# A normalised 3x3 convolution over 32 images: the order of work inside an image's slot, and the start of image 0

## The reference

```python
# x: (32, 128, 56, 56) float32; weight (128, 128, 3, 3); Wp, Wn: (1,); bias (128,)
w_norm = weight / max|weight|;  delta = 0.05 * max|w_norm|
tern = 1 where w_norm > delta, -1 where w_norm < -delta, else 0
wq = Wp * tern where tern > 0, Wn * tern where tern < 0, else 0
g = x in 32 groups of 4 channels, each normalised over its 4*56*56 values, eps 1e-5
out = x + conv3x3(g, wq, stride 1, padding 1) + bias
```

## Time and profile before

| | |
|---|---|
| median of 3 executions | 548.46 us (548.22 to 550.05) |
| the profiled execution | 549.22 us, span 547.5 us |
| busy, share of the span | TensorE 95%, VectorE 96%, ScalarE 87%, GpSimd 28% |
| transfers | 152.6 MB, mean 279 GB/s |
| image 0: sum complete on VectorE (second half of plane C) | 10.76 us |
| last store issued | 543.1 us |

### The profile page before, as it was taken

The page is one execution under the profiler, slowest core; times in us unless marked ns, Lnnn a source line. Parts: engine busy times, 40 slices in busy tenths (PEclk is TensorE's granted clock), DMA queues, the critical chain, the costliest instruction groups (busy, mean ns, idle before and its releaser), DMA issues. The chain is left out here.

```text
span 547.5 us, 9220 instructions
## 1 busy us (share of the span) xinstructions
PE 522.0 (95%) x3171; PEld 308.2 (56%) x3171; DVE 525.3 (96%) x448; ACT 475.8 (87%) x483; POOL 154.5 (28%) x138
## 2 busy tenths in 40 slices
PE   1898999999999999999999999999999999999995
PEld 0454655556555555655555555555555555555553
DVE  4999999999999999999999999999999999999985
ACT  2879999999989999899999999899998999999841
POOL 2313332232333223233322233322223332222320
PEclk9998999999999999999999999999999999999999
DMA  7535999999999999999999999999999999998766
GB/s 277 235 119 157 294 282 276 272 267 280 362 260 313 306 286 281 367 269 304 295 306 286 295 335 251 343 304 271 287 354 279 297 321 275 273 305 222 194 191 258
DMA packets 27959, 152.61 MB, mean 279 GB/s; under 512 B 3488, under 2 KB 3488, under 8 KB 27936
## 3 DMA queue, kind: packets, MB, share of 16 engines
q1 hardware_dynamic: 18576, 102.77, 48.3%
q0 software_dynamic: 8784, 48.98, 45.8%
q10 hardware_dynamic: 576, 0.59, 0.3%
HBM read 100.94 MB, written 51.38 MB: 278 GB/s over the span
## 5 line engine op out<-in xcount | busy, mean ns | idle before, releaser
L841 PE MATMUL even_rows<-parts,w_lhsT 128*128 128x392 f16 (+1 forms) x1536 | 265.8, 329 | 4.3 <-DVE parts L679 1.9
L841 PE MATMUL odd_rows<-parts,w_lhsT 128*128 128x392 f16 (+1 forms) x1536 | 263.3, 327 | 1.9 <-ACT d_sb L430 1.7
L841 PEld LDWEIGHTS even_rows<-parts,w_lhsT 128*128 128x128 f16 x1536 | 150.0, 99 | 105.9 <-issue 6.9
L841 PEld LDWEIGHTS odd_rows<-parts,w_lhsT 128*128 128x128 f16 x1536 | 147.3, 97 | 110.4 <-issue 11.8
L672 DVE SCALAR_TENSOR_TENSOR parts<-plane,norm_scale,parts 128x1568 f16<-128x1568 f32 x111 | 203.5, 1843 | 1.6 <-ACT parts L439 1.5
L349 POOL TENSOR_TENSOR plane<-x 128x756 f32<-128x756 f32 x64 | 97.4, 1522 | 343.3 <-DVE plane L609 115.9
L439 ACT ACTIVATE parts<-plane,norm_scale 128x1568 f16<-128x1568 f32 x111 | 177.7, 1601 | 9.2 <-ACT plane L473 4.9
L478 ACT ACTIVATE junk<-x,negmean 128x3136 f16<-128x3136 f32 x32 | 92.7, 2898 | 0.0
L424 ACT ACTIVATE c_sb<-even_rows,bias_sb,out_scale 128x1568 f32<-128x1568 f32 x32 | 53.1, 1659 | 15.9 <-PE even_rows L841 15.9
L387 POOL DMA_DIRECT2D y<-in_x_dram x61 | 54.2, 988 | 31.2 <-DVE y L689 29.4
L689 DVE SCALAR_TENSOR_TENSOR y<-odd_rows,out_scale,c_sb 128x1568 f32<-128x1568 f32 x31 | 57.4, 1853 | 2.2 <-issue 1.3
(11 more groups left out here) (67 smaller groups left out, 132.9 us busy)
## 6 DMA issues: line engine op xcount, KB each, us to landing
x<-in_x_dram SPq DMA_DIRECT2D x64, 784.0 KB, 12.0
out_dram<-y SPq DMA_DIRECT2D x63, 784.0 KB, 6.2
y<-in_x_dram POOLq DMA_DIRECT2D x61, 784.0 KB, 12.1
out_dram<-y SPq DMA_DIRECT2D x2, 392.0 KB, 3.7
y<-in_L_conv_weight_dram ACTq DMA_DIRECT2D x1, 576.0 KB, 6.5
wp_sb<-in_L_conv_Wp_dram ACTq DMA_DIRECT2D x1, 0.5 KB, 7.6
wn_sb<-in_L_conv_Wn_dram ACTq DMA_DIRECT2D x1, 0.5 KB, 7.9
bias_sb<-in_L_conv_bias_dram ACTq DMA_DIRECT2D x1, 0.5 KB, 7.8
```

The costliest lines, as they stand in the source:

```text
L841: ins = nc.tensor.matmul(product_ps(odd, b, b + 1)[:, 0, r0 - b * BANK_ROWS:r1 - b * BANK_ROWS, :], w_lhsT[:, prod, kh, :], part(img, prod ...
```

## The change

Every engine's slot gets another order, and slots -1 and 0 too.
- TensorE: the statistics matmul of n+1 (with the mean of n+2) moves from ahead of product C to between products D and A of slot n. It waits for the copy of C (`c_ready`), the squares of n+1 and the sum of n+2. Bank 3 of A waits for the root's and the mean's readers, no longer bank 3 of C.
- VectorE: the slot begins with low D of n (it was the last of slot n-1), then odd rows of n-1, low A, plane C of n+2 (it was of n+3), low B, reciprocal, D of n+1, Newton, A of n+1, scale, even rows of n, low C of n+1.
- ScalarE: squares of n+1, high B, copy of C, root of n+1, mean of n+2, copy of D, centre, high C, high D, edges and high A of n+1. The casts of the turned weights A and B move here from VectorE, into slot 0.
- GpSimd: the first half of plane B waits for plane A of that image alone; for image 0 for its sum instead of its root. The second half always waits for low D.
- Slot -1: the mean of image 1 gets a matmul of its own (`sum_second_mean`) behind the turned weights, so that the variance of image 0 no longer waits for plane C of image 1; only the weights C are turned ahead of it. The first half of plane D comes ahead of plane C of image 1, the output scales move to slot 0, the edges ahead of the root, and there are 7 warm-up matmuls instead of 6.

```diff
 PSUM_BANK = 512
-WARM_UP = 6
+WARM_UP = 7
...
@@ -351,27 +352,20 @@
         if h:
             ins.then_inc(plane_ready[B], 1)
-    def first_half_b(img, now, third):
+    def first_half_b(img, now):
         pool.wait_ge(x_loaded[img.buf], img.turn * 32 + 32)
         wait(pool, lo_ready[B], img.count())
         if now:
             wait(pool, product_done[A], now.half(1, 1, 1))
-            if now.j == 0:
-                pool.wait_ge(plane_ready[A], img.count(plus=1))
-            elif third:
-                pool.wait_ge(sum_ready, third.count(plus=1))
-            else:
-                pool.wait_ge(plane_ready[A], img.count(plus=1))
+            pool.wait_ge(plane_ready[A], img.count(plus=1))
         else:
-            pool.wait_ge(std_ready, img.count(plus=1))
+            pool.wait_ge(sum_ready, img.count(plus=1))
         difference_b(img, 0)
     def second_half_b(img, prev):
         if prev:
             wait(pool, product_done[B], prev.half(1, 1, 1))
-            pool.wait_ge(lo_ready[D], img.count(plus=1))
-        else:
-            pool.wait_ge(plane_ready[A], img.count(plus=1))
+        pool.wait_ge(lo_ready[D], img.count(plus=1))
         difference_b(img, 1)
...
         if nxt:
-            first_half_b(nxt, now, third)
-
-    slots(p, pool, emit, ahead=4)
+            first_half_b(nxt, now)
+
+    slots(p, pool, emit)
...
 nc.scalar.activation(root_of_zero[:], no_bias[:], ACT.Sqrt)
 def run(p):
+    def copy_turned_weights(js):
+        for j in js:
+            wait(act, product_done[j], p * N_IMG * HALVES)
+            act.wait_ge(w_turned, 4 * p + j + 1)
+            nc.scalar.activation(w_lhsT[:, j].rearrange("p k c -> p (k c)"), turned_ps(j),
+                                 ACT.Copy).then_inc(last_w_ready, 1)
+
...
             nc.scalar.activation(first_rows(part(img, C, HI), h), first_rows(plane_of(img, C), h), ACT.Copy,
                                  scale=norm_scale[:, b_slice(img)]).then_inc(ready, 1)
-    def take_mean(img):
-        if img.j == 0:
-            act.wait_ge(mean_summed, p + 1)
+    def take_mean(img, first=False):
+        if first:
+            act.wait_ge(mean_summed, 2 * p + img.j + 1)
...
@@ -490,43 +491,30 @@
     def emit(prev, now, nxt, far):
         first_slot, second_slot = not now and not prev, now and not prev
         if first_slot:
-            take_mean(nxt)
+            take_mean(nxt, first=True)
             sum_squares(nxt)
+            edges(nxt)
+            root(nxt)
             centre(nxt)
-            root(nxt)
-            take_mean(far)
-            edges(nxt)
             make_first_hi(nxt)
+            take_mean(far, first=True)
             make_hi(nxt, D)
-        elif second_slot:
-            sum_squares(nxt)
-            make_hi(now, A)
+        elif now:
+            if second_slot:
+                copy_turned_weights((A, B))
+                make_hi(now, A)
+            if nxt:
+                sum_squares(nxt)
+            make_hi(now, B)
             copy_c(now)
-            make_hi(now, B)
-            root(nxt)
-            take_mean(far)
-            copy_d(now)
-            centre(nxt)
-            make_hi(nxt, C)
-            make_hi(nxt, D)
-            sum_squares(far)
-            edges(nxt)
-            make_hi(nxt, A)
-        elif now:
             if nxt:
                 root(nxt)
             if far:
                 take_mean(far)
+            copy_d(now)
             if nxt:
                 centre(nxt)
-            make_hi(now, B)
-            copy_c(now)
-            if nxt:
                 make_hi(nxt, C)
-            if far:
-                sum_squares(far)
-            copy_d(now)
-            if nxt:
                 make_hi(nxt, D)
                 edges(nxt)
...
                             apply_absolute_value=True).then_inc(w_max_local, 1)
 def ternary_weights():
+    dve.wait_ge(scalars_loaded, 32)
+    nc.vector.tensor_tensor(equal[:], wp_sb[:], wn_sb[:], ALU.is_equal).then_inc(w_step, 1)
+    steps[0] += 1
     dve.wait_ge(w_max_turned, 1)
     step(nc.vector.tensor_reduce(w_max[:], w_max_ps, AX_X, ALU.max))
     nc.vector.tensor_scalar(above[:], w_max[:], THRESHOLD, None, ALU.mult)
-    nc.vector.tensor_scalar(below[:], w_max[:], -THRESHOLD, None, ALU.mult).then_inc(w_step, 1)
-    steps[0] += 1
-    dve.wait_ge(scalars_loaded, 32)
-    step(nc.vector.tensor_tensor(equal[:], wp_sb[:], wn_sb[:], ALU.is_equal))
+    step(nc.vector.tensor_scalar(below[:], w_max[:], -THRESHOLD, None, ALU.mult))
     step(nc.vector.tensor_scalar(neg, w_raw, below[:], equal[:], ALU.is_lt, ALU.mult))
     nc.vector.scalar_tensor_tensor(pos, w_raw, above[:], neg, ALU.is_gt, ALU.subtract).then_inc(w_ternary, 1)
...
@@ -726,61 +714,50 @@
             make_first_c(nxt, 1)
             if p == 0:
                 ternary_weights()
-                output_scales()
+            make_first_d(nxt, 0)
             make_c(far)
-            make_first_d(nxt, 0)
+            rstd_of_x(nxt)
             turned_weights((C, D))
-            rstd_of_x(nxt)
             make_first_d(nxt, 1)
             make_first_lo(nxt)
-        elif second_slot:
-            make_a(now)
+        elif now:
+            if second_slot:
+                make_a(now)
             make_lo(now, D)
-            turned_weights((A, B))
+            if prev:
+                output_rows(prev, ODD)
+            if second_slot and p == 0:
+                output_scales()
             make_lo(now, A)
-            make_c(far)
+            if far:
+                make_c(far)
+            if second_slot:
+                make_d(nxt)
             make_lo(now, B)
-            make_d(nxt)
-            first_rstd(nxt)
-            make_a(nxt)
-            newton_factor(nxt)
-            scale_of_x(nxt)
-            output_rows(now, EVEN)
-            make_lo(nxt, C)
-            make_lo(nxt, D)
-            make_c(third)
-        elif now and nxt:
-            output_rows(prev, ODD)
-            first_rstd(nxt)
-            make_lo(now, A)
-            newton_factor(nxt)
-            make_d(nxt)
-            scale_of_x(nxt)
-            make_lo(now, B)
-            make_lo(nxt, C)
-            make_a(nxt)
-            if third:
-                make_c(third)
-            output_rows(now, EVEN)
-            make_lo(nxt, D)
-        elif now:
-            output_rows(prev, ODD)
-            make_lo(now, A)
-            make_lo(now, B)
-            if p == 0:
-                add_half_residual(prev)
-            for odd in (EVEN, ODD):
-                add_last_residual(now, 0, odd)
-            last_output_rows(now, 0, 2, EVEN, first_rows_done[EVEN])
-            last_output_rows(now, 0, 2, ODD, first_rows_done[ODD])
-            for odd in (EVEN, ODD):
-                add_last_residual(now, 1, odd)
-            last_output_rows(now, 2, 3, EVEN, last_rows_done[EVEN])
-            last_output_rows(now, 2, 3, ODD, last_rows_done[ODD])
-            last_output_rows(now, 3, 4, EVEN, even_done)
-            last_output_rows(now, 3, 4, ODD, odd_done)
-
-    slots(p, dve, emit, ahead=4)
+            if nxt:
+                first_rstd(nxt)
+                if not second_slot:
+                    make_d(nxt)
+                newton_factor(nxt)
+                make_a(nxt)
+                scale_of_x(nxt)
+                output_rows(now, EVEN)
+                make_lo(nxt, C)
+            else:
+                if p == 0:
+                    add_half_residual(prev)
+                for odd in (EVEN, ODD):
+                    add_last_residual(now, 0, odd)
+                last_output_rows(now, 0, 2, EVEN, first_rows_done[EVEN])
+                last_output_rows(now, 0, 2, ODD, first_rows_done[ODD])
+                for odd in (EVEN, ODD):
+                    add_last_residual(now, 1, odd)
+                last_output_rows(now, 2, 3, EVEN, last_rows_done[EVEN])
+                last_output_rows(now, 2, 3, ODD, last_rows_done[ODD])
+                last_output_rows(now, 3, 4, EVEN, even_done)
+                last_output_rows(now, 3, 4, ODD, odd_done)
+
...
-    def sum_stats(img, ahead, start=True):
+    def sum_second_mean(img):
+        pe.wait_ge(sum_ready, img.count(plus=1))
+        nc.tensor.matmul(mean_ps, group_mean[:], sum_of(img), start=False, stop=True,
+                         skip_group_check=True).then_inc(mean_summed, 1)
+
+    def sum_stats(img, ahead, start=False):
         pe.wait_ge(sumsq_ready, img.count(plus=1))
         if ahead:
             pe.wait_ge(sum_ready, ahead.count(plus=1))
-            nc.tensor.matmul(stats_ps, group_mean[:], sums[:, img.buf, :], start=start, stop=True,
-                             skip_group_check=not start).then_inc(var_summed, 1)
-        else:
-            nc.tensor.matmul(var_ps, group_mean[:], sums[:, img.buf, 0:1], start=True,
-                             stop=True).then_inc(var_summed, 1)
+        to = stats_ps if ahead else var_ps
+        of = sums[:, img.buf, :] if ahead else sums[:, img.buf, 0:1]
```

(36 more changed lines are left out.)

1 line of the change is left out of this document (added).

## The result

The kernel after took 550.95 us (median of 7 executions, 550.05 to 551.77), the kernel before 548.26 us (7, 547.92 to 550.05) on the same chip: ratio 1.0044, 95% interval 1.0032 to 1.0057. The forecast was 546.3 us, 0.4% faster; it became 0.4% slower. The profiled execution of the kernel after took 551.69 us for a span of 550.1.

What follows compares the result with a forecast made beforehand. VectorE bound it at 15.94 us per image, TensorE just behind; image 2 at 55.2, plus 29 x 16.10, plus 1.3 gave 523.4, span 545.3, plus 0.96: 546.3 us, 0.4% faster. Likeliest 544.3 to 547.5, eight in ten 542.8 to 551.0.

Steps and rivals of the forecast that it cites:

- the tail: From image 31's first matmul to the end: hangs on product D and its copy, unchanged at 21.9 us.
- First matmul: Image 0's first product on TensorE: at about 20.65 instead of 21.65, as its first low half starts 1.0 us sooner.
- Threshold pass: VectorE's pass over the weights ahead of image 0: held by GpSimd to 12.3, 0.95 us later; bounds 0 and 1.2.
- GpSimd wins: After low D of image 0: GpSimd's second half of plane B goes first, low A starts at 26.4 instead of 25.1.
- may start fast: Product C of image 0, with the gap ahead closed: may be some 2 us shorter at 2.4 GHz; nothing booked.
- Period: Steady-state time per image: 16.06 to 16.13 us, taken 16.10 against 15.94; 6 loop turns at 0.22 add 1.3.
- VectorE's way: From the statistics matmul over scale, even rows, low C, then TensorE's products C and D: closes after 16.02 us.
- ScalarE's way: ScalarE's unbroken run from high C to the copy of C: closes at 16.04 to 16.06, 16.13 with a waited-for statistics matmul.
- Rivals 2 and 3: 2: chain has slack, VectorE bounds at 15.94, 541.7 us, chance 0.12; 3: chain longer, period 16.28, 551.5 us, chance 0.22.
- rival 4: Image 0: GpSimd shut out by VectorE until about 29.7, everything after slips 3.5 us, 549.8 us; chance 0.08.
- rival 5: Transfers are the real bound, so a faster start is lost in waits for loads; time as before; chance 0.04.
- the chain: Steady state: next image's statistics, between products D and A, wait for the copy of C and release all its work.

Runs made afterwards that it cites:

- the filling: Kernel after plus 22 matmuls of unused result in slot 0, between product D and the wait for the copy of C: 548.27 us, ratio 0.9985.
- old end: Kernel after with gap-filling matmuls; last slot's odd rows before low D, GpSimd's second half there not waiting for low D: 547.01 us, ratio 0.9966.
- both halves by VectorE: Kernel after with gap-filling matmuls and changed last-slot order; VectorE adds both halves of image 30's residual, no GpSimd transfer for it: 548.09 us, ratio 0.9987.
- plane D early: Kernel after with plane D of the next image ahead of low B in every slot, without gap-filling matmuls: 548.46 us, ratio 0.9991.
- the short edges: Kernel after with gap-filling matmuls; ScalarE's edge columns one row instead of 56 from image 1 on, output not the reference's: 544.92 us, ratio 0.9927.

## Why the prediction was wrong

The step that failed is the tail: "21.9 us again", with "Low D ahead of the odd rows delays these by 1.8 us, which VectorE had idle ahead of that copy." It took the end to hang on product D ("the copy of D and what follows hang on it"). VectorE did have the time: its last rows and the last store were no later. But the odd rows are read by somebody else. The residual waits for them, the stores of image 30 wait for the residual, and image 31's stores queue behind these. The prediction knew of it ("the residual and the store of an image start 2 us later in its slot") and covered it with "four output buffers behind them". In the last slot buffers cover nothing, since what counts is when the last byte lands. Measured: residual 1.3 us later behind image 31's first matmul, first store 1.0 to 1.6 later, and the end 23.3 to 25.1 us behind it in the six profiles that have the new last slot as it is, 21.9 to 22.2 in the four that have the old one. By the two kernels with the filling, on two chips, this is worth 1.0 to 1.3 us. There is a floor under it: with no stores queued up (old end, or both halves by VectorE) the last rows end the kernel, 4.4 to 5.2 us behind the last store.

The second failure is an omission. The prediction had both ends of TensorE's gap in slot 0 (product D done at "28.9 to 30.8", the statistics at 30.75) and booked nothing, as the copy of C sets the time in any case. The gap is harmless by itself. What it does to the matmuls behind it was not asked. In part of the executions the granted clock fell, product A took 1.7 us more, and VectorE waited 1.55 us for it. With the gap filled the median fell by 2.0 us, of which the part that no profile shows is named above. These two together explain the sign: 550.27 with both, 548.27 with the gap filled, 547.01 without either (ratios 1.0026, 0.9985, 0.9966), and the forecast was 546.3. Of the 3.2 us at the end in the first profile of the kernel after, some 1.6 are in one more of the six (plane D early, 25.0) and not in the other four; its last two stores took 6.8 us to land, against 5.2 with the filling. In these two profiles, and in none of the other ten, the trace has two 16 KB packets of the queue that the page calls "instruction" (q8) side by side, about 18.8 us behind image 31's first matmul, of about 1.6 and 1.9 us, and the last packets of the stores end at 23.7 us, in the other four of the six at 22.0 to 22.2. Whether they cause it is not shown.

Point by point:
- First matmul "at about 20.65": 20.69.
- Threshold pass "may start only at 12.3", 0.95 us: it started on time at 11.50 and took 1.68 instead of 0.88, ending at 13.18, 0.8 late. The size was right and the sign of it in the trace was not: a held-up instruction of VectorE shows as a longer one. Newton was released, 0.22. Low A of image 0 began at 25.10, took 2.97 and ended at 28.07; GpSimd was in its half from 24.95 to 26.42. "GpSimd wins" holds. By the Trainium skill's rule (SBUF — State Buffer, section Who interferes with whom), that the second to come waits, these rows agree, 0.88 to 1.68 and 1.85 to 2.97.
- That product C of image 0 "may start fast": it did, and that opened the gap. The prediction tied it to "the gap closed"; by the warm-ups the clock was already up ahead of the gap.
- Period: taken 16.10, bounds to 16.13; measured 16.12, with 16.03 ahead of each turn of the loop and 16.38 to 16.44 at it, so that a turn costs about 0.2 us net, 0.22 taken. The 29 images took 468.41, forecast 468.2. ScalarE's run and the 0.38 us of a waited-for statistics matmul are the last 0.1 us, shown by the short edges. VectorE's way turned out at 16.12 too, since that longer matmul is at its head as well; the prediction gave the 0.07 to ScalarE's way alone.
- Rivals 2 and 3 (a period of 15.94, or of 16.28) are excluded by the 16.12, rival 4 by GpSimd's second half of image 0, which had its turn at 24.95, rival 5 by the start, 3.5 to 6.5 us sooner by which profiles are compared, of which the steady state gave back only what its period says.

A version with the statistics ahead of the wait for the copy of C, which might open the chain, was not tried: its two columns lie in the bank that ScalarE is copying.

## What to carry to other kernels

In the last iteration every step has a reader that the steady state hides: book a moved output against the last transfer, not against the next use of its buffer. Follow the whole queue of each engine: once the odd rows were moved back, a wait that costs nothing in the steady state (low D in front of GpSimd's half) held up the residual, and TensorE's last products too. Profile the old kernel more than once before a gain is booked against it: its own start differed by 0.97 us. When one product gets faster and the next is released by something else, a gap appears on TensorE; ask what the granted clock does behind it, and put matmuls into it if it is short.

## What was not expected of the hardware

- Behind the same gap the clock falls in one execution and holds in another. Behind 1.74 us of idle the granted clock averaged 0.71 for 5.9 us in one profile of the kernel after and stayed at 1.00 in the other; behind 1.40 us it fell to 0.50 for 3.4 us in one profile of the kernel before and stayed at 1.00 in the other. With 0.60 us left of the gap, the clock and span of none of 12 executions showed the loss. What decides between them is open.
- A slow first product need not come from the gap ahead of it. Two gaps of 1.08 and 1.07 us were followed by product C in 4.09 and in 5.84 us; the seven warm-ups ahead of the gap had taken 1.53 us in the first case and 2.40 in the second.
- VectorE and GpSimd hold each other up both ways: the second half of plane B took 2.95 us instead of 1.47 where it met low A.
- A one-element reciprocal costs VectorE 0.08 us ahead of an instruction that doesn't read it, and 0.19 ahead of one that does.
